# First aggregation of a graph layer: the aggregate halved with nodes on partitions, four f16 squares turned, one ScalarE copy

## What is computed

```python
def _graph_conv(x, edges, W0, b0, W1, b1):
    src = concatenate([edges[:, 0], edges[:, 1]])
    dst = concatenate([edges[:, 1], edges[:, 0]])
    deg = maximum(segment_sum(ones_like(dst), dst, 6250), 1.0)
    agg = segment_sum(x[src], dst, 6250) / deg[:, None]
    return x @ W0 + b0 + agg @ W1 + b1

xn = layernorm(x)
h  = relu(_graph_conv(xn, edges, W0_0, b0_0, W1_0, b1_0))   # 256 -> 512
h  = _graph_conv(h, edges, W0_1, b0_1, W1_1, b1_1)          # 512 -> 256
x  = x + h + mix(xn)
x  = x + experts(layernorm(x))
```

## Time and profile before

| | |
|---|---|
| median of 3 runs | 2259.36 us (2257.18 to 2259.43) |
| profiled execution | 2261.03 us, its span 2259.5 us |
| busy in the span | PE 2077.5 us (92%), DVE 1553.7 (69%), ACT 1199.1 (53%), POOL 371.3 (16%) |
| first aggregation | about 370 to 1067 us |
| L2253 matmuls (both aggregations) | 4802, 1160.2 us |
| L1276 pairs | 1300, 452.0 us |

### The profile page before, as it was taken

How to read it: one execution, slowest core, us unless ns; L and a number is a source line. 1 busy time by engine, 2 the same in 40 slices (tenths; PEclk the granted TensorE clock), 3 DMA queues, 4 the chain that set the end, 5 groups by cost and what they waited for, 6 DMA issues and landing times.

```text
span 2259.5 us, 52353 instructions
## 1 busy us (share of the span) xinstructions
PE 2077.5 (92%) x15356; PEld 1308.7 (58%) x15357; DVE 1553.7 (69%) x4887; ACT 1199.1 (53%) x2466; POOL 371.3 (16%) x438
## 2 busy tenths in 40 slices
PE   3887789999999999999689989999999996999996
PEld 2676675555555555555345444444444443899996
DVE  6898987999999999998355544545455544465554
ACT  3677663555555555555465643444444443566664
POOL 2000000000000000000111111122111122366665
PEclk9999898999999999999899999999999997999998
DMA  3323237222222222223343426555555554565552
GB/s 93 89 86 98 79 99 205 115 115 115 115 115 115 115 115 115 115 115 135 106 163 118 140 102 239 200 191 195 190 196 203 201 194 153 145 96 93 88 93 42
DMA packets 158447, 299.12 MB, mean 132 GB/s; under 512 B 31614, under 2 KB 107695, under 8 KB 156131
## 3 DMA queue, kind: packets, MB, share of 16 engines
q1 hardware_dynamic: 130787, 243.66, 31.3%
q0 software_dynamic: 25856, 47.15, 9.5%
q10 hardware_dynamic: 1664, 6.35, 0.8%
HBM read 148.32 MB, written 144.19 MB: 129 GB/s over the span
## 4 chain that ended last, share of the span: by engine, by line
PE 71%; issue 10%; DVE 7%; DVEq 4%; POOLq 2%; DMA 2%; SPq 1%; POOL 1%; ACT 1%; ACTq 0%
PE bank L2253 46%; PE bank L2244 6%; PE bank L2469 6%; PE bank L2454 6%; POOLq L827 2%; DVEq L1148 2%; DVE big L1105 1%; DVE big L1118 1%; PE bank L2436 1%; DVEq L1114 1%; DVE big L1100 1%; PE bank L2261 1%; PE bank L2401 1%; DVE big L1116 1%; DMA big<-rows_dram 1%
## 5 line engine op out<-in xcount | busy, mean ns | idle before, releaser
L2253 PE MATMUL bank<-RW,big 128*128 128x512 f16 x4802 | 1160.2, 380 | 5.1 <-DMA big<-a_dram 4.9
L2253 PEld LDWEIGHTS bank<-RW,big 128*128 128x128 f16 x4802 | 436.4, 98 | 396.5 <-issue 10.0
L1902 ACT ACTIVATE big<-bank 128x512 f16<-128x512 f32 (+1 forms) x640 | 364.2, 573 | 316.6 <-PE bank L2244 316.6
L1276 DVE TENSOR_TENSOR big<-iotaB,keys 128x512 f16<-128x512 f16 x1300 | 452.0, 417 | 7.9 <-issue 7.0
L2244 PEld LDWEIGHTS bank<-big 128*128 128x128 f16 x2560 | 191.0, 98 | 106.2 <-issue 1.4
L2244 PE MATMUL bank<-big 128*128 128x128 f16 x2560 | 247.5, 219 | 0.5 <-issue 0.5
L959 POOL DMA_INDIRECT out_dram<-big x112 | 179.6, 1604 | 112.2 <-ACT big L2047 76.6
L895 POOL DMA_DIRECT2D big<-in_L_ffn_W_dram x8 | 6.4, 802 | 1054.1 <-DVE R L1335 1052.4
L2038 ACT ACTIVATE big<-bank,b1A,iscA 128x256 f32<-128x256 f32 x224 | 114.2, 561 | 100.1 <-PE bank L2454 96.8
L2469 PE MATMUL bank<-RW,big 128*128 (+1 forms) x1344 | 158.4, 275 | 0.5 <-DVE big L1699 0.5
L2454 PE MATMUL bank<-big,RW 128*128 128x256 f16 x1344 | 157.3, 274 | 0.4 <-ACT big L2027 0.4
(11 more groups left out here) (417 smaller groups left out, 2911.4 us busy)
## 6 DMA issues: line engine op xcount, KB each, us to landing
big<-a_dram SPq DMA_DIRECT2D x49, 800.0 KB, 6.1
big<-a_dram SPq DMA_DIRECT2D x49, 768.0 KB, 4.6
a_dram<-big SPq DMA_DIRECT2D x49, 640.0 KB, 3.0
a_dram<-big SPq DMA_DIRECT2D x49, 512.0 KB, 2.6
a_dram<-big SPq DMA_DIRECT2D x49, 416.0 KB, 2.4
big<-rows_dram SPq DMA_DIRECT2D x56, 265.0 KB
big<-in_x_dram SPq DMA_DIRECT2D x96, 128.0 KB, 2.1
own_dram<-big SPq DMA_DIRECT2D x48, 256.0 KB, 2.5
```

What stands on the lines that cost most here:

```text
L1276: last = v.tensor_tensor(out[q].rearrange("p b (m k) -> p b m k", k=2), inturn(iotaB[:, :], QB, P // 2), twice(kd[:, q * QB:(q + 1) * QB, ...
L1902: a.activation(Ab[q][:, 0:n], banks[BB(q)][:, 0:n], ACT.Copy).then_inc(s_ab, 1)
L2253: last = mm(bank[:, :], blk(q, c), R2[:, u * 2 * D:(u + 1) * 2 * D], start=(i == 0), stop=(i == T - 1))
```

## The change

VectorE splits `aggn` into its two f16 halves before the turning, with nodes on partitions, in `agg16`, which lies over `aggc`. TensorE turns four f16 squares instead of two f32 ones. `place1` goes from VectorE; instead ScalarE copies the turned halves from bank 6 to `R3h` with one instruction (`turned1`), ahead of `copy(t)`. As `agg16` lies over `aggc`, `finish1(t)` now also waits for the turning of tile t-1. Bytes, banks and the place in `R3h` are the same.

```diff
--- before.py
+++ after.py
@@ -292,6 +292,7 @@
         AB = [bigh[:, i * ABLK * P:(i + 1) * ABLK * P] for i in range(2)]
         aggr = sp3b.f32(2 * D)
         aggc = sp3b.f32(D)
+        agg16 = aggc.bitcast(F16)
         aggn = sp3b.f32(D)
         xres = sp3b.f32(D)
         x2n = sp3b.f32(D)
@@ -1320,20 +1321,19 @@
             def finish1(t):
 
                 dve.wait_ge(s_ag[0], t + 3)
+                if not isinstance(t, int) or t:
+                    dve.wait_ge(s_at, t)
                 v.scalar_tensor_tensor(out=aggc, in0=aggr[:, D:2 * D], scalar=1.0 / S, in1=aggr[:, 0:D],
                                        op0=ALU.mult, op1=ALU.add)
                 dve.drain()
                 v.scalar_tensor_tensor(out=aggn, in0=aggc, scalar=dg[:, 2:3],
                                        in1=R3[:, bass.ds(t * D, D)],
-                                       op0=ALU.mult, op1=ALU.add).then_inc(s_an[0], 1)
-
-            def place1(t):
-                dve.wait_ge(s_at, t + 1)
-                hi = R3h[:, bass.ds(t * 2 * D, D)]
-                v.tensor_scalar(hi, banks[6][:, 0:D], S, None, ALU.mult)
-                dve.drain()
-                v.scalar_tensor_tensor(out=R3h[:, bass.ds(t * 2 * D + D, D)], in0=banks[6][:, 0:D], scalar=S, in1=hi,
-                                       op0=ALU.mult, op1=ALU.subtract).then_inc(s_ac, 1)
+                                       op0=ALU.mult, op1=ALU.add)
+                dve.drain()
+                v.tensor_scalar(agg16[:, 0:D], aggn, S, None, ALU.mult)
+                dve.drain()
+                v.scalar_tensor_tensor(out=agg16[:, D:2 * D], in0=aggn, scalar=S, in1=agg16[:, 0:D],
+                                       op0=ALU.mult, op1=ALU.subtract).then_inc(s_an[0], 1)
 
             def finish2(t):
 
@@ -1543,10 +1543,7 @@
             finish1(0)
             with dve.Fori(1, T) as t:
                 tile1(t + 1, t)
-                place1(t - 1)
                 finish1(t)
-
-            place1(T - 1)
 
 
             def tile4(n, i):
@@ -1906,6 +1903,10 @@
                 act.wait_ge(s_an[L], t + 1)
                 a.activation(aggr, bank[:, :], ACT.Copy).then_inc(s_ag[L], 1)
 
+            def turned1(t):
+                act.wait_ge(s_at, t + 1)
+                a.activation(R3h[:, bass.ds(t * 2 * D, 2 * D)], bankh[6][:, 0:2 * D], ACT.Copy).then_inc(s_ac, 1)
+
             def deviation(t):
                 act.wait_ge(s_v2, t + 1)
                 a.activation(x2r, x2m[:, 1:2], ACT.Sqrt, bias=epsc[:, :]).then_inc(s_d2, 1)
@@ -1928,6 +1929,8 @@
                 if L == 0:
                     for q in range(Q):
                         evac(t + (q + LEAD) // Q, (q + LEAD) % Q)
+                    if not isinstance(t, int) or t:
+                        turned1(t - 1)
                 elif last:
                     deviation(last[0])
                     high2(*last)
@@ -1958,6 +1961,7 @@
                     raise2(T - 1)
 
             aggregate(0)
+            turned1(T - 1)
 
             def squares(e):
                 act.wait_ge(s_wl, 48 * e + 48)
@@ -2280,8 +2284,8 @@
                     pe.wait_ge(s_ac, t + 1)
                 else:
                     pe.wait_ge(s_hvec, 4 * t + 8)
-                for h in range(2):
-                    last = nc.tensor.transpose(banks[6][:, h * P:(h + 1) * P], aggn[:, h * P:(h + 1) * P], ident[:, :])
+                for h in range(4):
+                    last = nc.tensor.transpose(bankh[6][:, h * P:(h + 1) * P], agg16[:, h * P:(h + 1) * P], ident16[:, :])
                 last.then_inc(s_at, 1)
 
             def transposed2(t, par):
```

## The result

The changed kernel takes 2270.27 us, median of 5 runs (2268.68 to 2271.6), against 2259.36 us (5 runs, 2257.18 to 2260.03): ratio 1.0051, 95% interval 1.0039 to 1.0062, so 9 to 14 us slower. The forecast was 2267 (2259 to 2275), slower, by a loop through three engines.

The account below looks back on a forecast made before the run. TensorE (14.17 us a tile) and VectorE (14.20) bound the kernel before; after the change a 14.34 us loop would. 47 x 0.16 = 7.5 us plus 0.3 at the end gives +7.8, hence 2267 us, range 2259 to 2275.

Parts of the forecast that it names:

- loop through three engines: First aggregation: copy, finish1, pairs, spread, degrees, rest of the tile, back to copy, forecast at 14.34 us a tile.

Follow-up runs that it names:

- e1: The changed kernel with ScalarE's turned1 behind copy(t) instead of ahead of it: 2256.27 us, ratio 0.9998 to the kernel before.

## What to carry to other kernels

When two engines hand work to each other several times in a tile, sum the path from each wait around to itself, besides each engine's work. Here both engines had their old load, 14.17 and 14.18 us a tile, and the path through the third one, 14.39, set the time. An operation moved to an idle engine is not free if it stands ahead of something that the full engine waits for; look for a place behind it first (in e1 moving one call took back the whole loss). And what stands ahead of a wait on a nearly full engine is cover for it: taking it away can turn a late result into a stall.

## What the runs showed that was not expected

- A stall in TensorE's stream costs more than the stall: 0.16 us of waiting ahead of one matmul made each tile 0.22 longer, because the matmuls behind it started 0.07 later than in an unbroken stream. In the rows the next weight load is late by the same 0.07. Why it is was not tried by itself.
- With a wait of 0.16 us a tile the profile still had TensorE 100% busy; the distances of starts showed it, and the waits of the weight loads.
- The first turning came at 392.4 to 397.1 us in ten profiles, although the stages ahead of the first aggregation have the same code in all. The cause is open. It is the reason that spans are compared here only together with the pitch.
